# A post-norm attention and FFN layer: one Pool subtraction instead of two, and three kinds of background work given other steps

## The reference

```python
x = layernorm(x + attention(x)); x = layernorm(x + ffn(x))

Q = x @ Wq.T + bq; K = x @ Wk.T + bk; V = x @ Wv.T + bv      # heads of 16
Q, K = Q*cos + rot_half(Q)*sin, K*cos + rot_half(K)*sin      # rotary
w = softmax(Q @ K.T / 4)                                     # 4 query heads per K/V head
attn = w @ V;  attention = attn @ Wo.T + bo
ffn = (silu((x @ gate_w.T)*gate_s) * ((x @ up_w.T)*up_s)) @ down_w.T * down_s
```

## Time and profile before

| | |
|---|---|
| times of the three runs | 1116.03, 1117.24, 1118.92 us |
| profiled execution, its own time | 1116.03 us |
| its span | 1114.1 us |
| TensorE (PE) busy | 1063.2 us, 95% |
| VectorE (DVE) busy | 783.6 us, 70% |
| ScalarE (ACT) busy | 638.0 us, 57% |
| Pool busy | 204.8 us, 18% |
| granted TensorE clock, mean | 0.996 |

### The profile page before, as it was taken

The page is one execution under the profiler, slowest core; times in us unless marked ns, Lnnn a source line. Parts: engine busy times, 40 slices in busy tenths (PEclk is TensorE's granted clock), DMA queues, the critical chain, the costliest instruction groups (busy, mean ns, idle before and its releaser), DMA issues. The chain is left out here.

```text
span 1114.1 us, 14770 instructions
## 1 busy us (share of the span) xinstructions
PE 1063.2 (95%) x5660; PEld 533.9 (48%) x5660; DVE 783.6 (70%) x892; ACT 638.0 (57%) x1205; POOL 204.8 (18%) x173
## 2 busy tenths in 40 slices
PE   8999999999999999999999999999889999999995
PEld 3533333333333533333333333333336588888884
DVE  5889969997787799787888799999403435353534
ACT  2158867886686678676666778777652032222221
POOL 1151031233030400300010306646000100000002
PEclk9999999999999999999999999999999999999998
DMA  6074417515132521512140366610306111010001
GB/s 228 39 195 113 101 46 154 149 49 99 55 73 89 111 47 29 104 57 54 31 74 12 72 184 145 189 42 23 116 29 144 40 56 38 1 39 1 1 38 40
DMA packets 36587, 86.42 MB, mean 78 GB/s; under 512 B 12512, under 2 KB 12896, under 8 KB 34432
## 3 DMA queue, kind: packets, MB, share of 16 engines
q1 hardware_dynamic: 35936, 84.71, 28.9%
q10 hardware_dynamic: 576, 0.72, 0.2%
HBM read 48.71 MB, written 23.86 MB: 65 GB/s over the span
## 5 line engine op out<-in xcount | busy, mean ns | idle before, releaser
L437 DVE TENSOR_REDUCE nmx<-PSA 128x1 f32<-128x1024 f32 x512 | 600.2, 1217 | 95.0 <-PE PSA L426 94.8
L504 ACT ACTIVATE Bn<-PS 128x512 f32<-128x512 f32 x1024 | 529.1, 604 | 157.0 <-PE PS L498 156.4
L498 PE MATMUL PS<-Qt,Kt 50*128 50x512 f32 x1024 | 374.5, 446 | 31.1 <-ACT Bn L504 18.0
L426 PE MATMUL PSA<-Kt,Qt 48*128 48x512 f32 x1024 | 393.6, 463 | 2.6 <-DVE nmx L437 1.5
L498 PEld LDWEIGHTS PS<-Qt,Kt 50*128 50x128 f32 x1024 | 167.5, 184 | 331.8 <-ACT Bn L504 298.9
L518 PE MATMUL PV<-Bn 128*32 128x512 f32 x2048 | 272.8, 605 | 0.0
L426 PEld LDWEIGHTS PSA<-Kt,Qt 48*128 48x128 f32 x1024 | 165.7, 184 | 33.2 <-DVE nmx L437 15.0
L1027 PE MATMUL PSA<-x1Th,wr 128*128 128x512 f32 x344 | 136.1, 396 | 0.9 <-DVE sg L1047 0.5
L1027 PE MATMUL PSA<-x1Tl,wr 128*128 128x512 f32 x344 | 134.8, 392 | 0.0
L1047 DVE SCALAR_TENSOR_TENSOR sg<-PSA,us,sg 128x512 f32<-128x512 f32 x43 | 32.1, 748 | 135.0 <-ACT sg L1038 134.8
L1038 ACT ACTIVATE sg<-PSA,gs 128x512 f32<-128x512 f32 x43 | 29.5, 689 | 156.9 <-PE PSA L1027 156.9
(11 more groups left out here) (119 smaller groups left out, 662.1 us busy)
## 6 DMA issues: line engine op xcount, KB each, us to landing
Qt<-pscr SPq DMA_DIRECT2D x90, 128.0 KB, 5.4
A<-in_wf SPq DMA_DIRECT2D x11, 768.0 KB, 7.3
wr<-A SPq DMA_DIRECT2D x33, 256.0 KB, 2.7
pscr<-A SPq DMA_DIRECT2D x16, 512.0 KB, 3.6
vscr<-Bn SPq DMA_DIRECT2D x32, 256.0 KB, 2.0
Kt<-pscr SPq DMA_DIRECT2D x90, 64.0 KB, 2.8
A<-in_xT SPq DMA_DIRECT2D x4, 1024.0 KB, 7.5
A<-A SPq DMA_DIRECT2D x16, 256.0 KB, 3.7
```

The source lines that it names most:

```text
L426: r = pe.do(lambda e, h=h, p=p: e.matmul(ps[:, h, :], Qt[i][p:p + NC_, g % 2, 128 * qt:128 * qt + 128], Kt[i][p:p + NC_, 512 * h:512 * h + ...
L437: r_mxs[hh, s] = dve.do(lambda e: e.tensor_reduce(nmx[:, hh % 2, c0:c0 + 1], ps, AX.XY, ALU.max, negate=True), c_rel[s])
L498: r = pe.do(lambda e: e.matmul(PS2[:, c % 3, :], Kt[i][rows, 128 * kt:128 * kt + 128], Qt[i][rows, g % 2, 512 * qh:512 * qh + 512], start= ...
L504: r_exp[c] = act.do(lambda e: e.activation(Pb[c % NP_], PS2[:, c % 3, :], ACT.Exp, scale=0.25), c_exp)
```

## The change

Two edits. In `project`, the two Pool subtractions of 512 columns become one of 1024 columns, queued behind the second cast. Both casts stay, in the same two pieces (they are now two source lines, L291 and L293). In the tables, the three remaining pieces of `second` move from steps 1, 2, 3 to 2, 3, 4; the last three of `third` from 7, 8, 9 to 8, 9, 10; and `gather(2)` from step 13 to step 10 of pair 0.

```diff
-            for h in range(2):
-                c = slice(512 * h, 512 * h + 512)
-                r = act.do(lambda e, c=c: e.copy(qrot[:, c].bitcast(F32R), raw[:, c]), c_hm)
-                pool.wait(r)
-                r = pool.do(lambda e, c=c: e.tensor_tensor(raw[:, c], raw[:, c], qrot[:, c], ALU.subtract), c_rpp)
-                yield
+            act.do(lambda e: e.copy(qrot[:, 0:512].bitcast(F32R), raw[:, 0:512]), c_hm)
+            yield
+            r = act.do(lambda e: e.copy(qrot[:, 512:1024].bitcast(F32R), raw[:, 512:1024]), c_hm)
+            pool.wait(r)
+            r = pool.do(lambda e: e.tensor_tensor(raw, raw, qrot, ALU.subtract), c_rpp)
+            yield
             sp.wait(r)
             write_parts(b, m, i, qrots[i], qraw[i])
...
-        for w, g in ((1, second), (2, second), (3, second), (4, third), (7, third), (8, third), (9, third)):
+        for w, g in ((2, second), (3, second), (4, second), (4, third), (8, third), (9, third), (10, third)):
...
-                put(n, {0: 13, 6: 5}.get(n, 3), lambda n=n: gather(n + 2))
+                put(n, {0: 10, 6: 5}.get(n, 3), lambda n=n: gather(n + 2))
```

## The result

The changed kernel took 1125.48 to 1128.31 us in four runs, median 1126.72; the kernel before, in four runs beside it, 1116.03 to 1118.92, median 1117.03. The ratio is 1.0086, 95% interval 1.0064 to 1.0107. Forecast were 1118.8 us and a range up to 1120.7: wrong, since 9.7 us were lost where 1.6 were expected. A late transfer cost about what was forecast; a second stall, and the clock behind both, were not in the sum.

A forecast was written before the change was run, and what follows sets the result against it. TensorE was taken to bound the kernel. Subtraction 0, casts 0 and gather +1.6 us gave 1117.6 us against the profiled execution, 1118.8 us against the median of 1117.24; range 1116.2 to 1120.7 us.

The forecast's parts named there:

- What bounds the kernel: Attention steps: TensorE, busy 95%, sets the pace at 2.60 us a step; what makes it wait adds in full.
- The Pool subtraction alone, 0: Eight projections: one subtraction saves 0.18 us of Pool each, its low part completes 1.10 us later; effect 0.
- Casts and pieces of `second` one step later, 0: ScalarE's idle gaps of 0.54 us take the moved casts; Pool's rotation of third, 1.6 us later, stays hidden; effect 0.
- Casts of `third`, 0: End of step (0, 8): the 0.7 us TensorE wait stays; effect taken as 0, bounds -0.1 to +0.3 us.
- The gather past the exchange: SP's queue before step (1, 0): exchange's read queues behind the gather, TensorE stalls 0.4 to 2.7 us, taken 1.6.
- The rivals: Three alternatives: exchange does not queue, 1117.2 us, chance 0.25; long stall, 1121.0 us, 0.10; gain, 1115.9 us, 0.05.
- The slower one: Step (1, 0): exchange's write waits 6.60 us, TensorE stalls 3.8 us, time 1121.0 us; chance 0.10.
- The decision point given for it: Exchange's read issued at 109.6: from there the loss at step (1, 0) passes 3.35 us.

The follow-up runs named there:

- e7: Kernel before plus eight unneeded Pool operations, one in each step (m, 3), released ahead of VectorE's cast; 1128.55 us, ratio 1.0104.
- e6: Kernel before with only the two Pool subtractions made one; 1117.62 us, ratio 1.0000.
- e1: Changed kernel with gather(2) back in step 13, behind the exchange; 1122.75 us, ratio 1.0045 to the kernel before.
- e3: Changed kernel with gather(2) back in step 13 and Pool's subtraction of second and third behind VectorE's transposition; 1118.22 us, ratio 0.9988 to the kernel before.
- e4: Kernel before with only gather(2) moved to step 10; 1117.92 us, ratio 0.9988.
- e2: Changed kernel with Pool's subtraction of second and third waiting for VectorE's last transposition; 1122.89 us, ratio 1.0036 to the kernel before.
- e5: Kernel before with only the later steps of second and third, subtractions still halves, gather(2) in step 13; 1119.54 us, ratio 1.0013.

## Why the prediction was wrong, step by step

- **What bounds the kernel.** Right: TensorE sets the pace in the steps, and what made it wait came through to the end. In every row of the table the last shift is at least as large as the one at step (1, 3). What holds up VectorE need not reach TensorE, though: four of e7's eight collisions cost nothing.
- **The Pool subtraction alone, 0.** Right (e6: 1.0000), but the sentence that bounds it was wrong: "nobody else waits for these subtractions". I asked who waits for its result and not who needs what it holds while it runs. With the step of the next edit it holds up VectorE's cast.
- **Casts and pieces of `second` one step later, 0.** This is the step that failed first. I even worked out the subtraction's time there, 76.9 to 79.3, and used it only for the rotation behind it; the cast at 77.0 lay inside, in a row I had not listed. Measured: a cast of 2.34 us, 2.14 us of loss without the clock (e1), 4.9 with it in the first and third trace, 3.35 in the second. The trace of the kernel before had the sign of it: late in the span, two of its own casts are long and end with an operation of Pool, 765.84 + 0.71 = 766.55 against 765.24 + 1.28 = 766.52.

```profile
765.84 0.71 DVE L450 CAST msp<-nmx 128x16 fp32r<-128x16 f32 x1
```

```profile
765.24 1.28 POOL L843 TENSOR_TENSOR lowsum<-lowsum,lowf 128x512 f32<-128x512 f32 x1
```

- **Casts of `third`, 0.** Right: e3 keeps them and loses nothing.
- **The gather past the exchange, 0.4 to 2.7 us, taken 1.6.** The mechanism and the size of the wait were right. Taking out the 6.5 us by which this trace ran late, the exchange's write left at 103.2 (forecast 101.8 to 103.4), its read at 108.4 (106.7 to 108.9), and TensorE waited 2.15 us; in the four other traces with this order 2.21 to 2.36. I took the middle where the upper third was right: between write and read lay 5.24 to 5.43 us, more than the 4.49 of the earlier trace rows. It takes both, the order on SP and the later write of `third`: e4 has the order alone, e1 the later write alone, and neither waits there.
- **What a wait costs.** This failed as well, a term left out without a reason: the sum counted a stall of TensorE at its own length. Behind the exchange 1.2 us came on top in one trace, 2.3 in another, about 2.5 to 3.3 in the three of the changed kernel. This missing term is, in most traces, as large as the wait itself, and it applies to both stalls. Of the shift of 10.79 us in the third trace, 2.1 are the collision, 2.4 the late read, and 5.2 the running at 1.2 GHz behind the two, (5.08 - 0.17 - 2.14) + (9.89 - 5.08 - 2.36); 0.9 come later, from 680 us on, where Pool sums the low bits; that was not followed further.
- **The rivals.** The slower one ended on the right side, by the wrong road: its long wait of 6.6 us did not come. Its time of 1121.0 would have been short as well. The decision point given for it, the read's issue at 109.6, was not reached.

The rule on ring order in the Trainium skill, "DMA: Bandwidth & Descriptors", section "Queues, rings and completion order", cited for the gather, agrees with the 5.24 to 5.43 us between write and read; no run tells ring order from merely busy DMA engines. The rule on the shared ports in the Trainium skill, "SBUF — State Buffer", section "Who interferes with whom", spoke against this change and was not weighed.

## What to carry to other kernels

When an operation on Pool is moved or lengthened, lay its new interval over VectorE's timeline and look for copies, casts and operations with two inputs in SBUF, however small: here 0.17 us became 2.34. Before a gather is put ahead of a small urgent transfer on one queue, count from the small one's deadline backward, with the wait it has behind a full queue (4.8 to 5.4 us here) instead of on an empty one (2.0). And where TensorE sets the pace, give a new stall of it a price from its own length (1.5 to 2.4 us here) to a little over twice that, since the clock may fall behind it.

## What the runs showed of the hardware that was not expected

- The granted clock fell to 1.2 GHz at waits of 1.2 to 2.4 us, and once at one of 0.4: at their end or up to about 2 us later, for 3.4 to 13.7 us. It did so at all five late exchanges (the changed kernel's three traces, e2 and its repetition), behind three of four collisions of 2.34 us, behind the one of 1.25 us in e5, and behind one of sixteen of 1.64 us. What decides whether it falls is open. e1's collision, with a wait of 1.48 us, had none, 6 us behind the end of a low stretch; but e5 had such a stretch from 70 to 73 us and fell all the same. One execution of e2 took only 1118.61 us at a mean clock of 0.997, so the late exchange probably left the clock up there; it has no trace.
- It also falls without any of these: at 69 to 77 us, at the start of the steps, in four of the fourteen traces (e1, e4, e5 and the second one of e7), at 1.4 to 2.7 us each; at 46 to 50 us in the first trace of the changed kernel, its first 1.6 us of shift; and in e3 from 686 to 697 us, for about 4.5 us. In e3, VectorE's subtraction behind the cast (L454 there), with both inputs in SBUF, had just taken 1.24 us instead of 0.17, beside one of Pool's sums of the low bits (681.42 + 1.24 = 682.66, 681.36 + 1.28 = 682.64); whether that set it off is not shown. Falls of the clock go with the scatter of single executions: of the kernel before, those of 1121 us and more had a mean clock of 0.989 to 0.991, those under 1117 us one of 0.996 or 0.997.

```profile
681.42 1.24 DVE L454 TENSOR_TENSOR msp<-nmx,msp 128x16 fp32r<-128x16 f32 x1
```
